# Half of each expert's first low parts on GpSimd, and VectorE's gates behind group 0

## What is computed

```python
probs = softmax(logits); top_p, top_i = top_k(probs, 2)      # logits = layernorm(x) @ router
h     = silu(x @ w_a[e]) * (x @ w_b[e])                      # inner product of expert e
out   = sum over the two chosen e of  gate_e * (h @ w_y[e])
x     = x + tanh(g_ffn) * out
```

## Time and profile before

| | |
|---|---|
| median, lowest, highest of 3 runs | 2113.2, 2110.46, 2119.68 us |
| profiled execution, first to last instruction (span) | 2099.3 us |
| median of the runs less this span | 13.9 us |
| TensorE matmul busy | 1928.3 us (92%) |
| VectorE busy | 1026.6 us (49%) |
| ScalarE busy | 845.0 us (40%) |
| GpSimd busy | 657.1 us (31%) |

### The profile page before, as it was taken

One profiled execution on the slowest core, in us unless ns is written; L12 is line 12 of the kernel. 1 busy time (PEld: TensorE's weight loads), 2 busy tenths in 40 slices (PEclk: granted clock), 3 DMA queues, 4 the chain that ended last, 5 costly groups with the idle time before them and its releaser, 6 DMA issues. The chain is left out here.

```text
span 2099.3 us, 35633 instructions
## 1 busy us (share of the span) xinstructions
PE 1928.3 (92%) x12328; PEld 1568.3 (75%) x12328; DVE 1026.6 (49%) x2245; ACT 845.0 (40%) x1792; POOL 657.1 (31%) x551
## 2 busy tenths in 40 slices
PE   4889999999999999999859999999997895999994
PEld 3577878777777878787748888888885675999983
DVE  6324555555555555544464233333336566554564
ACT  3233443444434434334435233333322544555550
POOL 4011020303020110300023455554433204688872
PEclk9899999999999999999969999999998996999997
DMA  7630101010110201000044233333348216454546
GB/s 209 200 130 1 53 15 53 19 53 11 37 35 9 63 9 53 19 17 18 5 152 137 57 110 110 105 110 120 109 143 263 101 58 202 147 200 152 209 146 202
DMA packets 113526, 201.58 MB, mean 96 GB/s; under 512 B 33135, under 2 KB 33935, under 8 KB 112867
## 3 DMA queue, kind: packets, MB, share of 16 engines
q1 hardware_dynamic: 108579, 183.94, 27.3%
q0 software_dynamic: 4800, 15.73, 2.3%
HBM read 171.65 MB, written 27.99 MB: 95 GB/s over the span
## 5 line engine op out<-in xcount | busy, mean ns | idle before, releaser
L461 POOL TENSOR_TENSOR a_rows<-a_rows,a_gain_x 128x512 f32<-128x512 f32 (+1 forms) x48 | 69.3, 1443 | 555.7 <-DVE a_rows L876 555.7
L620 PE MATMUL a_kv_ps<-a_kvin_hi,a_wk_hi 128*128 128x512 f32 (+1 forms) x512 | 196.0, 383 | 1.0 <-DVE a_kvin_lo L883 1.0
L1094 PE MATMUL f_banks<-f_wab_hi,f_x_hi 128*128 x448 | 183.8, 410 | 0.7 <-DVE f_x_lo L1781 0.7
L621 PE MATMUL a_kv_ps<-a_kvin_lo,a_wk_hi 128*128 128x512 f32 (+1 forms) x512 | 180.3, 352 | 0.0
L622 PE MATMUL a_kv_ps<-a_kvin_hi,a_wk_lo 128*128 128x512 f32 (+1 forms) x512 | 180.2, 352 | 0.0
L1096 PE MATMUL f_banks<-f_wab_hi,f_x_lo 128*128 x448 | 176.8, 395 | 0.0
L1095 PE MATMUL f_banks<-f_wab_lo,f_x_hi 128*128 x448 | 176.1, 393 | 0.0
L543 ACT ACTIVATE a_probs<-a_probs,a_neg_max 100x822 f32<-100x822 f32 x128 | 125.9, 984 | 113.1 <-DVE a_neg_max L907 112.9
L1803 DVE TENSOR_TENSOR f_h_sb<-f_h_sb,f_banks 128x256 f32<-128x256 f32 x112 | 47.2, 421 | 240.6 <-ACT f_h_sb L1526 239.6
L1526 ACT ACTIVATE f_h_sb<-f_banks 128x256 f32<-128x256 f32 x112 | 43.1, 385 | 290.5 <-PE f_banks L1096 290.5
L620 PE MATMUL a_kv_ps<-a_wv_hi,a_kvin_hi 128*128 128x512 f32 (+1 forms) x384 | 156.6, 408 | 1.0 <-DVE a_k_lo L900 1.0
(11 more groups left out here) (411 smaller groups left out, 4874.9 us busy)
## 6 DMA issues: line engine op xcount, KB each, us to landing
f_raw<-f_pieces SPq DMA_DIRECT2D x94, 256.0 KB, 2.7
m_raw<-m_pieces SPq DMA_DIRECT2D x92, 256.0 KB, 2.9
f_wab_raw<-f_pieces SPq DMA_DIRECT2D x42, 512.0 KB, 6.2
m_wab_raw<-m_pieces SPq DMA_DIRECT2D x42, 512.0 KB, 6.6
a_rows<-ctx SPq DMA_DIRECT2D x8, 1280.0 KB
ahead_piece<-g_ctx SPq DMA_DIRECT2D x2, 2880.0 KB, 20.1
a_wout_sb<-L_xattn_Wkv SPq DMA_DIRECT2D x8, 512.0 KB, 14.6
m_y_acc<-m_pieces SPq DMA_DIRECT2D x8, 512.0 KB, 5.9
```

The source lines that it names most:

```text
L461: own.link(nc.gpsimd.tensor_tensor(row, row, gain_x[0:n, :], ALU.mult))
L620: nc.tensor.matmul(out, hi_l, hi_r, start=first, stop=False)
L621: nc.tensor.matmul(out, hi_l, lo_r, start=False, stop=False)
L1094: nc.tensor.matmul(out, left_hi, right_hi, start=start, stop=False)
```

## The change

`MINE = PER // 2` inner pieces of each expert in group 0 stay with VectorE (2 of 4 in `f`, 1 of 2 in `m`); the others, eight in each layer, go to GpSimd, which makes them ahead of its gathers. VectorE's list of own pieces is 8 long; it makes four ahead of L1773 as before, then two, `x_lo` of tile 0, two, `x_lo` of tile 1, and goes into group 0. The gates come behind group 0, and the reading of the number of tiles in use comes behind the last group. TensorE waits for both counters.

```diff
+    MINE = PER // 2
-            return g == 0 and c < LAST or g == G - 1 and c >= PIECES - SHARED
+            return g == 0 and c < LAST and c % PER < MINE or g == G - 1 and c >= PIECES - SHARED
-        POOL_FIRST = PIECES - LAST
+        POOL_FIRST = PIECES - E * MINE
 ...
+            low_weights(0, 0, LAST)
             pool.wait_ge(rows_done, 1)
             gather_rows(0)
             pool.wait_ge(expert_done, 2)
             used = pool.value_load(...)
-            low_weights(0, 0, G * PIECES)
+            low_weights(0, LAST, G * PIECES)
 ...
-                        pe.wait_ge(wlo_dve[q], LOW0 + PER + PER * experts[s])
+                        pe.wait_ge(wlo_dve[q], LOW0 + MINE + MINE * experts[s])
+                        pe.wait_ge(wlo_pool[q], LOW0 + PER - MINE + (PER - MINE) * experts[s])
 ...
-            for c in range(AHEAD):
+            own_first = [c for c in range(LAST) if by_dve(0, c)]
+            for c in own_first[:AHEAD]:
                 split(0, 0, c)
 ...
-            for c in range(AHEAD, LAST):
+            for n, c in enumerate(own_first[AHEAD:]):
                 split(0, 0, c)
-                if c == AHEAD + 3:
+                if n == 1:
                     low_tokens(0, 0)
-                if c == AHEAD + 5:
-                    low_tokens(0, 1)
+            low_tokens(0, 1)
+            group(0, 0, True)
             dve.wait_ge(exp_done, 1)
             ... the gates, unchanged ...
+            for g in range(1, G):
+                group(0, g, False)
             dve.wait_ge(expert_done, 2)
             used = dve.value_load(...)
-            for g in range(G):
-                group(0, g, g == 0)
```

More of the change, by code:

```diff
@@ L1834, in _ @@
             dve.sem_inc(gates_done, 1)
+            for g in range(1, G):
+                group(0, g, False)
             dve.wait_ge(expert_done, 2)
             used = dve.value_load(expert[0:1, SLOTS:SLOTS + 1], min_val=0, max_val=SLOTS)
-            for g in range(G):
-                group(0, g, g == 0)
             with dve.If(used > CORE):
                 dve.wait_ge(add_done[0], ADD0 + CORE * G)
-                for c in range(LAST):
+                for c in own_first:
                     split(1, 0, c)
```

## The result

The changed kernel took 2134.19 us (median of 4, 2133.14 to 2139.96) beside 2112.64 us for the kernel before: ratio 1.0117, 95% interval 1.01 to 1.0135. That is 21.5 us more, where 11.6 were forecast. Two later comparisons gave 1.0095 (1.007 to 1.012) and, on a chip where the kernel before took only 2102.9 us, 1.0062 (1.0049 to 1.0075), which is +14.3 us. Why the same change is worth 14 or 21 us is the main thing that the experiments found.

A forecast was written before the change was run, and what follows sets the result against it. TensorE, never idle from the first inner product on, was taken to bound the kernel by its start and few waits. `f` +6.7 and `m` +4.9 gave +11.6 on 2113.2: 2124.8 us, 8-in-10 range 2113 to 2129.

The forecast's parts named there:

- `f`, start of the inner product: Front of `f`: routing held beside GpSimd's subtractions +7.3 us, earlier `x_lo` -0.6, together +6.7.
- `m`, start of the inner product: Front of `m`: routing held +7.4 us (bounds 0 and 10.1), earlier `x_lo` of tile 0 -0.4.
- The routing held by turns: VectorE's routing ahead of the gathers waits for whole GpSimd subtractions: +7.3 us in `f`, +7.4 in `m`.
- The replay: Turn-by-turn reckoning of VectorE beside GpSimd: `f`'s row marks begin 7.3 us later; gates make TensorE wait 1.8 to 3.1.
- What `x_lo` was to save: Tile 0's `x_lo` comes behind two splits instead of four: 0.6 us less in `f`, 0.4 in `m`.
- The waits of group 0 in `m` go: TensorE's waits of 2.49 and 0.57 us and the slow clock go; -5.0 with `x_lo` (bounds -3.1 to -5.9).
- The gates behind group 0: Behind group 0 of `m`, gates delay tile 0's product and TensorE waits: +2.5 us (bounds 0.3 and 5.3); `f` 0.
- 13.9 under the median of the runs, which lies around the span and is not touched: Profiled execution of 2099.3 us plus an untouched 13.9 gives 2113.2, to which the change adds +11.6.
- Small ones not held: Rival: GpSimd does not hold the routing's small instructions; -3.7 us, 2109.5 us, chance 0.13.
- Turns not strict: Rival: VectorE gets two or three short instructions between two of GpSimd; delays halve, +2.9, 2116.1 us, chance 0.17.
- The clock falls behind new waits: Rival: clock falls in group 0 of `m` (+1.57) and behind the gates (+1.57); 2127.9 us, chance 0.15.

The follow-up runs named there:

- before_third: The kernel before, unchanged, profiled a third time, on a chip without late signals: 2102.68 us, span 2101.0.
- after_third: The changed kernel, unchanged, a third time, on a chip without late signals: 2117.24 us, span 2114.0, ratio 1.0062 to the kernel before.
- before_again: The kernel before, unchanged, profiled a second time: 2113.04 us, span 2111.3, with late signals.
- after_again: The changed kernel, unchanged, run again beside the kernel before: 2133.05 us, ratio 1.0095.
- four_in_f: Against the changed kernel: GpSimd makes four low parts instead of eight ahead of the gathers in `f`, `m` as in the change; 2129.64 us, ratio 1.008.
- memset: Against the changed kernel: each of GpSimd's eight early subtractions replaced by two zero fills, which read nothing from SBUF; 2117.58 us.
- pool_only: Against the changed kernel: gates and register back ahead of group 0, GpSimd's early low parts kept; 2124.02 us, ratio 1.0061.
- The plain pair: The kernel before and the changed one, each with plain copies of 128 rows instead of gathers: 2408.98 and 2425.54 us, with other outputs.
- dve_gap: Against the kernel before: gates moved to VectorE's wait for the first gather, register behind the last group; run twice, 2113.42 and 2112.76 us, ratios 1.0002 and 1.0.
- spaced_again: Against the kernel before: a GpSimd fill between each two gathers, on a chip with late signals; 2103.81 us, ratio 0.9955.
- spaced: Against the kernel before: a GpSimd fill between each two gathers, on a quiet chip; 2105.99 us, ratio 1.0011.

## Why the prediction was right or wrong

The terms, with what each measured in us, quiet (before_third against after_third) and with late signals (before_again against after_again). The start of the inner product is counted from the layer's first fill on GpSimd.

| step | forecast | quiet | late signals |
|---|---|---|---|
| `f`, start of the inner product | +6.7 | +6.1 | +6.3 |
| `f`, from there to its end | 0 | -1.4 | +2.1 |
| `m`, start of the inner product | +7.0 | +7.0 | +7.1 |
| `m`, group 0 | -4.6 | -5.4 | -0.3 |
| `m`, group 1 (gates) | +2.5 | +5.0 | +5.0 |
| all else | 0 | +1.7 | +0.4 |
| span | +11.6 | +13.0 | +20.6 |
| medians of the runs beside them | +11.6 | +14.3 | +21.3 |

"All else" is no effect of the change: in the quiet pair it is -2.3 us ahead of layer `f`, +4.7 between the layers and -0.7 behind `m`, stretches that hold nothing of the edit but the moved register load. In the 20 profiles `f`'s first fill lies anywhere from 1065.2 to 1072.1 us. So a pair of profiles can be read stretch by stretch, but its whole is uncertain by a few us.

*The routing held by turns: right in kind, and in size although its parts were off.* The first gathers came 6.7 to 7.0 and 7.3 to 7.5 us later in the three profiles of the change, against 7.3 and 7.4, and dose (four_in_f), removal of the reads (memset) and isolation (pool_only) all agree. The replay had GpSimd beside all nine instructions of `f`, for 7.3 us, and none beside the row marks. But GpSimd stops for its high parts, so in the first profile six of the nine were held, 5.2 us, and the marks took 2.0 more. The total came out because each of the eight subtractions held one step, whichever it was; the split was wrong. What `x_lo` was to save, 0.6 and 0.4, was 0.6 and 0.5 in the quiet pair.

*The waits of group 0 in `m` go, -4.6 of the -5.0: right in a quiet execution, absent with late signals.* -5.4 with the clock at 1.00; -0.3 with late signals, since then ScalarE gets TensorE's signals up to 12 us late and sets the pace, whatever VectorE has ready.

*The gates behind group 0, +2.5: right place, half the size.* The wait was 3.0 us, inside the 1.8 to 3.1 of the replay. The slow clock behind it, which the rival priced at 1.57 and the forecast left out, cost 2.0.

*The step that failed* is the one that joined trace and median: "13.9 under the median of the runs, which lies around the span and is not touched". It is touched. In every other profile the time is 1.7 us above the span, so only 1.7 of the 13.9 lay around it, and 12.2 inside. Of the 12 us between the first and second span of before, 7.5 are group 0 of `m` and 2.2 group 0 of `f`: late signals in just the stretch that the change works on. So a gain computed in the quiet trace could not be had in those runs: of the 9.7 us that are missing between +11.6 and +21.3, 4.3 are group 0 of `m`, 2.5 the gates, 2.1 group 0 of `f`, and the rest is under 1 us a row.

The first profile was probably not one of the runs beside it at all. Its time would be 2101.0 us; none of the 63 runs of before beside kernels with late signals (the four of the first comparison among them) is under 2108.28, while the 40 on the two quiet chips lie from 2095.62 to 2111.82. The record does not say on which chip it was taken.

With +5.0 for the gates a quiet sum would have been +14.1. The plain pair has that inside the two layers (14.1). The quiet pair has 11.3 there, 13.0 in its spans and 14.3 in its medians (10.3 to 15.8), so that its nearness to 14 owes something to the stretches outside the layers.

*The rivals.* "Small ones not held" fell with 1.24 us for 16 numbers. "Turns not strict" fell too, since every step held beside a subtraction was held to its end; the three of the nine that were free in `f` fell into GpSimd's pauses. It is true in another sense: rarely, one engine waits through a whole row of the other's. "The clock falls behind new waits" was half right, behind the gates.

Left open: why after the change group 0 of `f` lasts 71.6 and 72.5 us with late signals and 69.0 and 68.4 without the change (TensorE idle 3.2 and 3.9 us of it against 1.8 and 1.1; pool_only 67.3, dve_gap 70.2 and 67.3: it varies), and what makes a signal late. The eleven profiles with late signals and gathers 1.25 us apart have 674 to 753 fewer records of signals than the 14,790 that the quiet ones of both kernels have, so recording and lateness go together. They do so in place as well: from the first gather of a layer to 3 us after its last, before_again has 220 records in the two layers, where before_third has 633; spaced_again has 664 there, where the quiet spaced has 709, and misses its other 370 outside the gathers. The Trainium skill, "NOTIFIC — the notification-queue block", section "Interfaces", says that a full internal buffer of that block can stall an engine. No run here shows that it was this, nor whether an execution that is not recorded has late signals.

## What to carry to other kernels

Before giving work to an idle GpSimd, look at what VectorE does at that time: if it is a chain of short instructions with SBUF inputs, each of GpSimd's reading instructions costs the chain its whole length, however small the held one is; the traces show PSUM inputs and reductions free of it. (Moving the work into the idle stretch, between the gathers, gained nothing here either: 1.0012 and 1.0018.) And before working from one trace, compare its span with the runs: a gap of 0.6% was not noise to be added at the end, but 12 us, most of it in two stretches. A second profile of the kernel before, beside those runs, shows it. Where ScalarE waits for "remote" behind a TensorE that has finished, try spreading the indirect DMAs that run then; on a chip without late signals that cost 0.1%.

## What the runs showed of the hardware

- Held for a whole GpSimd subtraction (1.26 us of two SBUF inputs): 16 numbers on one partition (TENSOR_SCALAR, 0.16 to 1.24 us), 128x8 (TENSOR_TENSOR, 0.17 to 1.00 us). Not held: an input in PSUM (0.17), TENSOR_REDUCE (0.19).
- Beside a GpSimd fill, instructions with two SBUF inputs keep their time (2.36 us for the row marks), while TENSOR_SCALAR is held until the fill ends (0.45 instead of 0.18 us).
- The exchange is not always one for one. VectorE waited 8.56 and 8.31 us through the rest of a row of subtractions without a gap, once each in 2 of 20 profiles; GpSimd waited once through a row of four splits (3.17 us instead of 1.27).
- Signals of TensorE can reach ScalarE up to 12.0 us late (9.6 to 12.0 at the second Silu of `m`) while indirect gathers are issued every 1.25 us: in eleven of the twelve profiles taken beside a kernel before of 2112 to 2113 us, the twelfth being its own first, whose chip is not on record; and in neither of the two taken beside one of 2103. At 1.65 to 1.8 us apart none was late on such a chip. The cause is open.
- A wait of 3.0 us on TensorE behind group 0 of `m` cost 2.0 us more through the clock (group 1 at 0.96 instead of 1.00, with 0.50 for 2 us of it).
